# A vision-transformer block on one core: the expert layer's second product with its tokens stationary

## The reference

```
h = tok(x)                                    # 3x3 filters made per pixel by a small network
h = h + attention(layernorm(h))               # 1 head, width 64, 4096 keys of each image
h = h + ffn(layernorm(h))                     # top-1 of 32 experts, hidden width 16

# ffn, for each token n:
idx = argmax(xf @ router_w.T + router_b)
hid = relu(xf @ W1[idx] + b1[idx])            # 16 values
out = relu(hid @ W2[idx] + b2[idx])           # 64 values
```

## Time and profile before

| | us |
|---|---|
| median of 3 runs | 1134.55 (1134.44 to 1134.91) |
| the profiled execution's own time | 1132.9 |
| its span, first to last instruction | 1131.0 |
| TensorE busy (matmuls) | 1097.7 (97%) |
| ScalarE busy | 628.4 (56%) |
| VectorE busy | 491.2 (43%) |

### The profile page before, as it was taken

How to read it: one execution, slowest core, us unless ns; L and a number is a source line. 1 busy time by engine, 2 the same in 40 slices (tenths; PEclk the granted TensorE clock), 3 DMA queues, 4 the chain that set the end, 5 groups by cost and what they waited for, 6 DMA issues and landing times.

```text
span 1131.0 us, 29094 instructions
## 1 busy us (share of the span) xinstructions
PE 1097.7 (97%) x12634; PEld 555.7 (49%) x12634; DVE 491.2 (43%) x1101; ACT 628.4 (56%) x698; POOL 10.5 (1%) x35
## 2 busy tenths in 40 slices
PE   6699999999999999999999999999999999999996
PEld 1233344555544555555555555555555555555542
DVE  6788766437072552626346181633413040301323
ACT  2356656556566465655646555564655556465551
POOL 3000000000000000000000000000000000000000
PEclk9799999999999999999999999999999999999997
DMA  5645612113005120212104021040000000000000
GB/s 152 144 116 123 150 42 57 39 39 76 2 14 132 39 67 11 57 42 67 39 12 97 13 64 30 11 95 11 11 3 11 2 11 1 11 2 10 2 2 20
DMA packets 15346, 51.62 MB, mean 46 GB/s; under 512 B 2846, under 2 KB 6046, under 8 KB 14828
## 3 DMA queue, kind: packets, MB, share of 16 engines
q1 hardware_dynamic: 15212, 49.68, 19.1%
HBM read 41.77 MB, written 4.75 MB: 41 GB/s over the span
## 4 chain that ended last, share of the span: by engine, by line
PE 94%; DVE 2%; DMA 1%; ACT 1%; issue 1%; DVEq 0%; SPq 0%; ACTq 0%
PE z_ps L671 39%; PE scores L660 38%; PE both L627 4%; PE both L642 4%; PE both L519 2%; PE both L623 1%; DMA filter_ring<-filters 1%; PE both L650 1%; PE both L567 1%; PE both L557 1%; PE both L607 1%; PE both L588 1%; PE both L598 1%; PE both L634 0%; PE scores L547 0%
## 5 line engine op out<-in xcount | busy, mean ns | idle before, releaser
L881 ACT ACTIVATE probs<-scores 128x1024 f32<-128x1024 f32 x504 | 488.6, 1021 | 427.0 <-PE scores L660 427.0
L660 PE MATMUL scores<-g_t,keys_t 64*64 64x512 f32 x4096 | 516.0, 594 | 1.9 <-ACT g_t L860 1.2
L671 PE MATMUL z_ps<-probs,keys 64*64 64x512 f32 x4096 | 512.8, 590 | 0.0
L660 PEld LDWEIGHTS scores<-g_t,keys_t 64*64 64x64 f32 x4096 | 219.7, 134 | 228.6 <-issue 222.3
L671 PEld LDWEIGHTS z_ps<-probs,keys 64*64 64x64 f32 x4096 | 205.0, 133 | 183.2 <-issue 178.9
L1148 DVE COPY o_sb<-both 128x512 f32<-128x512 f32 x14 | 9.7, 691 | 319.8 <-PE both L642 319.8
L1048 DVE TENSOR_TENSOR hres<-hres,tap_product 128x504 f32<-128x504 f32 (+1 forms) x128 | 89.1, 696 | 11.2 <-issue 0.9
L1043 DVE SCALAR_TENSOR_TENSOR tap_product<-filter_ring,w,xin 128x504 f32<-128x504 f32 (+1 forms) x120 | 89.0, 742 | 8.0 <-DMA filter_ring<-filters 4.6
L627 PE MATMUL both<-y_t,w 64*64 64x512 f32 x464 | 64.3, 597 | 0.0
L873 ACT ACTIVATE hidden<-both 128x1024 f32<-128x1024 f32 (+1 forms) x58 | 58.5, 1008 | 6.5 <-PE both L627 6.5
L642 PE MATMUL both<-hidden,w 64*64 64x512 f32 x448 | 56.9, 592 | 0.0
(11 more groups left out here) (137 smaller groups left out, 565.6 us busy)
## 6 DMA issues: line engine op xcount, KB each, us to landing
filter_ring<-filters SPq DMA_DIRECT2D x90, 384.0 KB, 5.2
out_dram<-out_sb SPq DMA_DIRECT2D x32, 128.0 KB, 2.4
xin<-x_dram SPq DMA_DIRECT2D x6, 528.0 KB, 9.0
g_t<-g_t SPq DMA_DIRECT2D x24, 128.0 KB, 4.8
hidden<-once_dram SPq DMA_DIRECT2D x1, 930.0 KB, 13.3
hidden<-once_dram SPq DMA_DIRECT2D x1, 576.0 KB, 5.3
filters<-filters_sb SPq DMA_DIRECT2D x30, 18.0 KB
xin<-x_dram SPq DMA_DIRECT2D x1, 384.0 KB, 6.3
```

Source lines behind the costliest of these rows:

```text
L660: last = T.matmul(scores[rows_of(h), c, r * 512:(r + 1) * 512], keys_t[rows_of(r), i // NQ % 2, k * 128 + 64 * h:k * 128 + 64 * h + 64], g ...
L671: last = T.matmul(z_ps[rows_of(c), h, :], keys[rows_of(h), i // NQ % 2, 2 * k + r, :], probs[rows_of(h), (2 * g + c) % RING, r * 512:(r + ...
L881: A.activation(probs[:, unit % RING, :], scores[:, c, :], ACT.Exp, scale=first_scale[:, 0:1] if n == 0 and g <= ASKED else SCALE).then_inc ...
```

## The change

The second product changes its roles: 64 tokens of `hidden` are stationary, and 64 columns of W2 move. So do the bias's: 64 tokens of the one-hot choice are stationary, and b2 moves. The result has tokens in partitions, as the output wants it, and `fin` is gone with its 16 matmuls. VectorE's two instructions of `fin` now follow its add in `o2`, read `o2_sb`, and the place in PSUM is released behind them. `o2` now has 32 bf16 and 128 float32 matmuls of 64 moving columns, and waits for all four `hid` before the first of them, and again before the second half. In the diff, `usual_groups` stands for all the plans: `fin` leaves `third_groups`, `fourth_groups` and `last_groups` in the same way. The last part is VectorE's `drain`.

```diff
 def usual_groups(n):
-    groups = merged({-1: at(m, "z"), 1: at(m - 1, "fin"), 2: at(m, "pz"), ...
+    groups = merged({-1: at(m, "z"), 2: at(m, "pz"), ...
...
             def store_block(m):
-                fin = f"fin@{m}"
-                sp.wait_ge(drained[places.of[fin]], places.nth[fin])
+                o2 = f"o2@{m}"
+                sp.wait_ge(drained[places.of[o2]], places.nth[o2])
...
                 elif name == "o2":
-                    for part in range(2):
-                        for r in range(2):
-                            T.matmul(mine[rows_of(r), r, :], b2_parts[rows_of(r), part, :], onehot_t[rows_of(r), :],
-                                     start=(part == 0), stop=False)
-                    for f in range(FT):
-                        wait_drained(f"hid{f}@{i}")
-                        if i == BLOCKS - 1:
-                            pe.wait_ge(upper_hidden, f + 1)
-                        for h in range(2):
-                            for r in range(2):
-                                last = T.matmul(mine[rows_of(r), h, :], w2[rows_of(h), f, :], hidden[rows_of(h), f, r, :],
-                                                start=(f == 0 and h != r), stop=(f == FT - 1))
-                    last.then_inc(done, 1)
-                else:
-                    wait_drained(f"o2@{i}")
-                    for j in range(4):
-                        for r in range(2):
-                            for h in range(2):
-                                last = T.matmul(both[rows_of(h), r, j * 64:(j + 1) * 64],
-                                                o2_sb[rows_of(r), j * 128 + h * 64:j * 128 + h * 64 + 64],
-                                                ident[rows_of(r), rows_of(r)], start=True, stop=True)
+                    for r in range(2):
+                        for f in range(FT):
+                            wait_drained(f"hid{f}@{i}")
+                            if i == BLOCKS - 1:
+                                pe.wait_ge(upper_hidden, f + 1)
+                        for j in range(BT // 2):
+                            at_tile = slice((r * BT // 2 + j) * D, (r * BT // 2 + j + 1) * D)
+                            tokens = [slice(j * 128 + 64 * h, j * 128 + 64 * h + 64) for h in range(2)]
+                            for part in range(2):
+                                for h in range(2):
+                                    T.matmul(mine[rows_of(h), r, at_tile], onehot_t[rows_of(r), tokens[h]],
+                                             b2_parts[rows_of(r), part, :], start=(part == 0), stop=False)
+                            for f in range(FT):
+                                for h in range(2):
+                                    for u in range(2):
+                                        last = T.matmul(mine[rows_of(h), u, at_tile],
+                                                        hidden[rows_of(u), f, r, tokens[h]], w2[rows_of(u), f, :],
+                                                        start=(f == 0 and u != r), stop=(f == FT - 1))
                     last.then_inc(done, 1)
...
-                    V.tensor_tensor(o2_sb[:, :], o2_sb[:, :], mine[:, 1, :], ALU.add).then_inc(done, 1)
-                else:
+                    V.tensor_tensor(o2_sb[:, :], o2_sb[:, :], mine[:, 1, :], ALU.add)
+                    settle()
                     if i > 1:
                         dve.wait_ge(out_stored[i % 2], 32 * (i // 2))
                     for r in range(2):
                         by_half = [...]
-                        last = V.scalar_tensor_tensor(by_half[0], both[:, r, 0:256].rearrange("p (j w) -> p j w", w=D),
-                                                      0.0, by_half[1], ALU.max, ALU.add)
+                        last = V.scalar_tensor_tensor(
+                            by_half[0], o2_sb[:, r * 256:(r + 1) * 256].rearrange("p (j w) -> p j w", w=D),
+                            0.0, by_half[1], ALU.max, ALU.add)
                     last.then_inc(done, 1)
```

More of the change, by code:

```diff
@@ L139, in third_groups @@
             5: at(0, "hid1"), 6: at(0, "hid2"), 7: at(0, "hid3"), 8: at(1, "yt"), 9: at(0, "o2"), 10: at(1, "lg"),
-            11: at(6, "xt"), 12: at(6, "g"), 13: [*at(1, "ot"), *at(7, "sum0 sum1")], 14: at(0, "fin"),
+            11: at(6, "xt"), 12: at(6, "g"), 13: [*at(1, "ot"), *at(7, "sum0 sum1")],
             15: at(1, "hid0"), 16: at(1, "hid1")}
@@ L145, in fourth_groups @@
     return {-1: at(2, "z"), 0: at(1, "hid2"), 1: at(1, "hid3"), 2: at(2, "pz"), 3: at(1, "o2"), 4: at(7, "sum2"),
-            5: at(2, "yt"), 6: at(2, "lg"), 7: at(1, "fin"), 8: at(7, "xt"), 9: at(7, "g"),
+            5: at(2, "yt"), 6: at(2, "lg"), 8: at(7, "xt"), 9: at(7, "g"),
             10: [*at(2, "ot"), *at(8, "sum0 sum1")], 11: at(2, "hid0"), 12: at(2, "hid1"), 13: at(2, "hid2"),
@@ L154, in usual_groups @@
     pair = {4: at(j, "cc"), 7: at(j, "cv")} if j in PAIRED else {}
-    groups = merged({-1: at(m, "z"), 1: at(m - 1, "fin"), 2: at(m, "pz"), 4: at(i, "sum2"), 5: at(m, "yt"), 6: at(m, "lg")}, pair,
+    groups = merged({-1: at(m, "z"), 2: at(m, "pz"), 4: at(i, "sum2"), 5: at(m, "yt"), 6: at(m, "lg")}, pair,
                     {8: at(i, "xt"), 9: at(i, "g"), 10: [*at(m, "ot"), *at(j, "sum0 sum1")]})
@@ L166, in last_groups @@
     return merged({-1: at(m, "z"), 2: at(m, "pz"), 3: at(m - 1, "hid0 hid1 hid2 hid3 o2"), 5: at(m, "yt"), 6: at(m, "lg"),
-                   7: at(m - 1, "fin"), 8: at(m, "ot"), 9: at(m, "hid0 hid1 hid2 hid3"), 15: at(m, "o2"),
-                   16: at(m, "fin")})
+                   8: at(m, "ot"), 9: at(m, "hid0 hid1 hid2 hid3"), 15: at(m, "o2")})
 def whole_plan():
@@ L969, in _ @@
             V = nc.vector
-            MINE = ("tap", "pz", "o2", "fin")
+            MINE = ("tap", "pz", "o2")
             def settle():
```

## The result

The changed kernel takes 1178.17 us (median of 4 runs, 1174.75 to 1180.37), against 1134.49 us for the kernel before (1134.39 to 1134.91). The ratio is 1.0386, with a 95% interval of 1.0358 to 1.0414: 44 us slower, where no change that can be told was forecast. The profiled execution took 1174.75 us, with a span of 1172.8.

The account below looks back on a forecast made before the run. TensorE's fills were taken to bound the long stretch. A gain of 2.5 us there and 0.9 us lost at the end gave -1.6 us, 1134.55 to 1133.0 us, no change that can be told; range 1129.6 to 1143.5.

Parts of the forecast that it names:

- What bounds the kernel: Long stretch, 61 to 1091 us: TensorE busy for all 1030.2 us, so each microsecond of its fills counts.
- Cost of the old and of the new form: TensorE, each block: old o2 and fin 4.33 us; new o2 3.99 to 4.30, taken as 4.10, 4.15 with waits.
- the bias: In new o2: 0.31 us a block if the free quarters go on, 0.62 if they stand still; taken nearer the first.
- Waits in it: Four long-fulfilled waits before o2's second half: between 0 and 0.56 us, taken as 0.05.
- Instructions: TensorE's code supply: 220 more load and matmul pairs a block, costed at nothing because code is fetched ahead.
- The worst case named: Code supply in o2: a fetch of 2.4 us would come 0.6 us late at worst, twice in a block.
- The end: Blocks 14 and 15: +0.4, +1.0, +0.3 and -0.8 us, a sum of +0.9 us.
- The burst isn't fed: Middle of each o2: instructions run short during waits or code fetches, so the kernel gets slower, 1142.9 to 1150 us; chance 0.19.
- Its first form, the waits: Middle of o2: whole 0.56 us pause and bias quarters standing still, +0.53 us a block, 1142.9 us with the end.
- its second, the code: In o2: two code fetches each 0.6 us late in every block, 17 us over the forecast, 1150 us.
- Small matmuls in a long row run at the slow pace: In o2: 29 ns a record gives 1192 us; a serial 25 ns a record gives about 1176; chance 0.06.
- VectorE's later release: Place `both`: where VectorE is behind, the next fill waits up to 0.84 us; 1145 us if in all blocks; chance 0.05.

Follow-up runs that it names:

- the paired bias: The one with the old form at the end, with the bias of both row halves r issued together for each piece pair: 1137.13 us, ratio 1.0021.
- the one with the old form at the end: Changed kernel with o2 of blocks 0 to 13 moved to the following attention block in four parts, old o2 and fin in the last two: 1142.42 us.
- the last kernel: The paired bias, with o2's four piece pairs two each in groups 0 and 1 of the attention block, except blocks 4, 8 and 12: 1132.93 us.

## Why the prediction was wrong

**What bounds the kernel:** right. TensorE's time decided everything in the long stretch, and no other engine is named for more than 0.9 us.

**Cost of the old and of the new form:** nearly right. The new o2 without a pause takes 4.36 to 4.40 us, where 4.15 was taken and 3.99 to 4.30 bounded it; 58 ns for a float32 record of a quarter held, from bursts of 32 to bursts of 256 (219 to 222 ns mean duration, as before). The term that was off is the bias: I took it that the free quarters mostly go on, from one row. They don't go on far: 0.62 for quarters that stand still gives 4.30, and the paired bias, which by these rows would have saved 0.31 then, saved 0.28 us a block. Instead of a gain of 2.5 us the layout alone costs about 1.

**Waits in it:** right at 0.05, as far as can be told. Taking them out moved nothing.

**Instructions:** this step failed. It said "I cost that at nothing, as the code is fetched ahead". It also worked out that o2 uses a block of code in 1.8 us and that a fetch may take 2.4, then didn't follow its own sum. Fetched ahead it is, but not far enough: bursts of 256 instructions never ran dry, bursts of 384 did at times and of 512 or more every time. This fits one block in stock ahead of the one in use. From a packet's start to the end of a pause in o2 it took 2.2 to 2.7 us in the changed kernel's trace. The worst case named, 0.6 us twice in a block, is by chance near what o2 itself lost: 14.8 us of pauses in 14 blocks, 1.06 each, mostly one pause of 0.7 to 1.5 us. What it left out is 7.0 us of pauses right behind o2, 0.22 us of latency with each pause, the slow clock, and the end stretch. The Trainium skill, "Runtime: NRT & Kernel Launch", section Instruction fetch mechanics, says that code is refilled in blocks of 256 instructions, that crossing one is mostly hidden, and that TensorE has room for 2048. The refill in 256 fits the 16 KB packets here. Hidden it isn't at this pace, and a stock near 2048 doesn't go with pauses in bursts of 384. The measurement decides. The same section of the Trainium skill also speaks of a store of only two blocks of 16 KB. The bursts here fit that.

**The branch:** missing. No step asked what stands behind o2. The three branches were there before and cost nothing. The branch instruction took 0.32 to 0.35 us then, and 1.16 to 3.33 right behind the burst. That it is reached earlier and with a full stock when long matmuls stand ahead of it is argued, not tried by itself. Behind the burst the pauses were 0.7 to 3.0 us each, and once a 3.4 us stretch at 1.2 GHz. Moving o2 away from them gave back 11.3 us, with the pauses in the bursts kept.

**The end:** the terms worked out gave 0.9 us, where 2.0 are left once the pauses are taken off. The same supply took 6.4 us more and 0.9 in latencies, since two pauses in each of the last two o2 stand on the chain.

**The rivals:** "The burst isn't fed" was the right one, with 0.19 and a price of 1143 to 1150. Its first form, the waits, was wrong; its second, the code, was right and too cheap. "Small matmuls in a long row run at the slow pace" had two prices, 1192 us and, as an estimate for a serial 25 ns a record, about 1176. The second is nearer to the 1178.17 measured than any other number of the prediction, and it is false all the same: a piece of 36 records takes 0.545 us, 15.1 ns a record, mean durations stayed at 219 to 222 ns and the clock at 1.00. A time that comes out near a rival's is no proof of it. VectorE's later release isn't felt: the one wait of 0.7 us put down to its L1154 is at the branch of block 8, where the scores start 0.46 us behind the end of the branch, as in blocks 4 and 12.

**What stays open.** How many instructions are in stock was only bounded. Block 0 takes 67.9 us in the one trace of the kernel before, 67.1 in the changed one, and 70 to 72 in the experiments, also where its code is unchanged. The traces show a difference in the clock: from 57 to 67 us its mean is 0.83 and 0.84 in the first two, 0.57 to 0.75 in the others, and block 0 takes 71 us and more where it is 0.62 or less. The same stretch in the kernel before and in the one with the old form at the end:

```profile
57.00:67.00 10.00, 9.68 (x76) 3.19 (x80) 8.89 (x14) 5.16 (x6) 0.00 (x0) 0.83 0.56 143
57.00:67.00 10.00, 7.75 (x72) 3.10 (x76) 8.82 (x15) 3.65 (x4) 0.00 (x0) 0.57 0.35 79
```

So 2 to 4 us of the experiments' times may have nothing to do with o2; why the clock stays down longer wasn't tried. Runs of the kernel before, beside all the experiments, spread over 1132.1 to 1136.2 us.

## What to carry to other kernels

When matmuls are made smaller, count instructions for each microsecond as well as columns: a burst of more than 256 loads and matmuls at some 7 ns each could outrun the supply of code here, however well the array was used, and every pause fell on a busy TensorE. The cure cost nothing: issue the small matmuls in portions between long ones, and keep them away from branches and from the end. With all of o2 spread over one group, 256 instructions last for some 3 us (an estimate from the counts), and some pauses were left; over two groups, as in most blocks of the last kernel, they last for some 4 us, and none was. If a price was worked out against a term that was set to zero, keep it in the sum.

## What the runs showed of the hardware

- In the long stretch a burst of 256 instructions of TensorE at about 7.3 ns each had no pause in 14 of 14 cases; of 384, four of 14 paused visibly (0.95 to 1.57 us); of 512, all 14 (0.90 to 1.48 us); of 576, all 14 as well, some with a second pause in or right behind o2.
- Float32 matmuls of 64 x 64 against 64 columns keep 14.5 ns a record for as long as code is there, with or without accumulation into the same columns.
- Quarters of the array run apart only a little: with bf16 work on two of them, the other two lost most of that time.
- A branch over untaken code took 0.32 to 0.35 us behind long matmuls and TensorE never stood still for it. Behind a burst of small ones it took up to 3.4 us, with pauses of up to 3.6 us.
